# A closing quantisation of y in two engine passes a block instead of four, with other places for the input rows

## What is computed

```python
QMAX, EPS = 7, 1e-8
def fp4_activation(x):
    scale = jnp.max(jnp.abs(x)) / QMAX + EPS
    q = jnp.clip(jnp.round(x / scale), -QMAX, QMAX) * scale
    return x + stop_gradient(q - x)

c = einsum('bct,bcd->bdt', x, w[conditions])      # 128 batches
h = gelu(ternary_linear(c, W1, b1))               # 512 -> 2048
y = ternary_linear(h, W2, b2)                     # 2048 -> 512
out = x + fp4_activation(y)
```

## Time and profile before

| | us |
|---|---|
| median of 3 runs | 1052.09 |
| lowest and highest run | 1050.0, 1052.19 |
| span of the profiled execution | 1048.1 |
| busy in it: PE, DVE, ACT, POOL | 938.5, 668.6, 574.4, 157.7 |
| DMA over the span | 77.89 MB, 74 GB/s on average |
| start of the closing part (first roundings) | 982.2 |

### The profile page before, as it was taken

How to read it: one execution, slowest core, us unless ns; L and a number is a source line. 1 busy time by engine, 2 the same in 40 slices (tenths; PEclk the granted TensorE clock), 3 DMA queues, 4 the chain that set the end, 5 groups by cost and what they waited for, 6 DMA issues and landing times.

```text
span 1048.1 us, 15055 instructions
## 1 busy us (share of the span) xinstructions
PE 938.5 (90%) x5265; PEld 449.2 (43%) x5265; DVE 668.6 (64%) x1029; ACT 574.4 (55%) x721; POOL 157.7 (15%) x213
## 2 busy tenths in 40 slices
PE   0599999999999999999999999999999999999300
PEld 0355444444444444444444444444444444444100
DVE  3599766666566756576666666665666656532698
ACT  3489382827455463728273645647382827354495
POOL 4032303030211203030303011020303030000000
PEclk9899999999999999999999999999999999999755
DMA  6510120301111112102020111121210301115898
GB/s 218 200 44 4 36 56 11 81 10 40 46 44 42 48 40 50 40 25 65 10 66 23 41 45 45 40 50 40 48 42 10 80 10 40 40 40 188 297 384 333
DMA packets 40480, 77.89 MB, mean 74 GB/s; under 512 B 3840, under 2 KB 4240, under 8 KB 39952
## 3 DMA queue, kind: packets, MB, share of 16 engines
q1 hardware_dynamic: 36192, 73.47, 23.9%
q0 software_dynamic: 4096, 3.94, 1.3%
q10 hardware_dynamic: 176, 0.27, 0.1%
HBM read 60.89 MB, written 16.78 MB: 74 GB/s over the span
## 4 chain that ended last, share of the span: by engine, by line
PE 76%; issue 11%; DVE 7%; ACT 2%; POOL 2%; DMA 1%; SPq 0%; POOLq 0%; DVEq 0%; ACTq 0%
PE ps L427 38%; PE ps L439 35%; PE ps L415 2%; DVE wts L947 1%; DVE y L941 1%; PE ps L457 1%; ACT y L636 1%; POOL ws L339 1%; DVE st L697 1%; DMA yx<-in_x 1%; DVE y L937 1%; DVE y L811 0%; DVE wts L808 0%; DMA condb<-in_itok_B 0%; DVE yc L947 0%
## 5 line engine op out<-in xcount | busy, mean ns | idle before, releaser
L427 PE MATMUL ps<-yc,wts 128*128 128x512 f16 x2048 | 447.3, 379 | 0.3 <-ACT g L568 0.3
L439 PE MATMUL ps<-wts 128*128 128x512 f16 x1920 | 419.3, 379 | 0.7 <-ACT wts L592 0.7
L427 PEld LDWEIGHTS ps<-yc,wts 128*128 128x128 f16 x2048 | 199.6, 98 | 238.5 <-ACT g L568 0.8
L439 PEld LDWEIGHTS ps<-wts 128*128 128x128 f16 x1920 | 185.8, 98 | 220.4 <-ACT wts L592 0.9
L730 DVE SCALAR_TENSOR_TENSOR wts<-g,st,wts 128x512 f16<-128x512 f32 x256 | 186.4, 749 | 143.5 <-ACT wts L573 141.8
L568 ACT ACTIVATE g<-ps,b1t,st 128x512 f32<-128x512 f32 x256 | 197.9, 773 | 116.7 <-PE ps L427 106.4
L573 ACT ACTIVATE wts<-g,st 128x512 f16<-128x512 f32 x256 | 181.0, 713 | 0.0
L555 ACT ACTIVATE xs<-yx,st 128x2048 f16<-128x2048 f32 x28 | 56.1, 2002 | 144.2 <-DVE st L765 144.2
L361 POOL PARTITION_ALL_REDUCE st<-st x46 | 21.5, 468 | 669.5 <-DVE st L699 414.3
L339 POOL DMA_INDIRECT wg<-in_L_cond_weights,ids x112 | 106.6, 952 | 41.3 <-issue 28.3
L735 DVE SCALAR_TENSOR_TENSOR y<-ps,st,b2b 128x512 f32 (+1 forms) x56 | 41.9, 748 | 77.8 <-PE ps L439 77.8
(11 more groups left out here) (127 smaller groups left out, 431.9 us busy)
## 6 DMA issues: line engine op xcount, KB each, us to landing
yx<-in_x SPq DMA_DIRECT2D x56, 512.0 KB, 6.0
wts<-in_x SPq DMA_DIRECT2D x9, 1024.0 KB, 8.1
out<-wts SPq DMA_DIRECT2D x6, 1024.0 KB, 6.3
y<-in_L_ffn_W SPq DMA_DIRECT2D x8, 512.0 KB, 8.8
y<-in_L_ffn_W SPq DMA_DIRECT2D x4, 1024.0 KB, 8.0
out<-wts SPq DMA_DIRECT2D x8, 512.0 KB, 5.1
xs<-in_x SPq DMA_DIRECT2D x2, 1024.0 KB, 5.9
yc<-in_x SPq DMA_DIRECT2D x2, 1024.0 KB, 7.8
```

Source lines behind the costliest of these rows:

```text
L427: last = nc.tensor.matmul(psH[:, j % HB, :], T1T[:, k, j * P:(j + 1) * P], csp[:, a, k, :], start=(k == 0 and a == 0), stop=(k == KT - 1 a ...
L439: last = nc.tensor.matmul(psY[:, r % 2, :], hsp[:, a, j, r * P:(r + 1) * P], T2T[:, j, :], start=(j == 0 and a == 0), stop=(j == HT - 1 an ...
```

## The change

The rounded number y*qi + MAGIC, seen as bits, has the whole number q in two's complement in its low 16 bits, as MAGIC's own bits there are zero. The changed kernel reads those 16 bits directly in the final sum, as an int16 at every second place of `y`, so that `whole` and `clipped` go. The clip to 7 goes too: y/scale can't be over 7, since scale is max|y|/7 + EPS. What remains are `rounded` and `added`, with int16 in place of fp16 as `added`'s first operand, at a step of two.

Around it:

- Pieces: block 0 in four quarters (one tile of 512 each), block 1 in two halves, blocks 2 to 15 whole; 20 pieces. VectorE rounds the pieces 0, 1 and 3, ScalarE all others.
- Places: blocks 6 to 11 get the parts of `wts` in another order. Block 6's is free after one quarter of the last product and its load is issued then; 7 and 8 after two, 9 after three, 10 and 11 after all, as before. `APART` is (6, 8, 9, 11).
- Blocks 12 to 15 get places of their own, the y of blocks 0 to 3. SP issues the load of block b + 12 right behind the last store of block b; the wait for a landing is gone.
- One counter `o_stored` for all stores, waited for at the end.
- The memset of `magn` at the kernel's start is gone.

```diff
-        HALVED = (0, 1, 2)
-        PIECES = [(b, slice(m, m + 1)) for b in HALVED for m in (0, 1)] + [(b, slice(0, 2)) for b in range(len(HALVED), NB)]
-        BY_VECTOR = [1, 3, 5, 6] + list(range(8, len(PIECES), 3))
+        ALL = slice(0, 2)
+        CUT = {0: [(slice(m, m + 1), slice(n, n + 1)) for m in (0, 1) for n in (0, 1)],
+               1: [(slice(m, m + 1), ALL) for m in (0, 1)]}
+        PIECES = [(b, m, n) for b in range(NB) for m, n in CUT.get(b, [(ALL, ALL)])]
+        LAST_OF = {b: i for i, (b, _, _) in enumerate(PIECES)}
+        BY_VECTOR = (0, 1, 3)
...
+        def q_piece(b, m, n):
+            return y_piece(b, m, n).bitcast(I16).rearrange("p m n (t w) -> p m n t w", w=2)[:, :, :, :, 0]
+
+        def x_piece(b, m, n):
+            return xtail[b][:, m, n, :]
...
-        xtail += [parts[:, w, 0:2, :, :] for w in range(3)]
-        xtail += [parts[:, 0:2, 2, :, :], parts[:, 0:2, 3, :, :], parts[:, 2, 2:4, :, :]]
+        xtail += [parts[:, 0:2, 0, :, :], parts[:, 2, 0:2, :, :], parts[:, 0:2, 1, :, :]]
+        xtail += [parts[:, 0:2, 2, :, :], parts[:, 2, 2:4, :, :], parts[:, 0:2, 3, :, :]]
+        APART = (6, 8, 9, 11)
         XS = len(xtail)
-        APART = (9, 10)
+        xtail += [place(y[:, b, :, :].rearrange("p r t -> p (r t)")) for b in range(NB - XS)]
...
+            sp.wait_ge(quarters_used, 1)
+            load_tail(6)
             sp.wait_ge(quarters_used, 2)
-            for b in range(6, 9):
-                load_tail(b)
+            load_tail(7)
+            load_tail(8)
...
-            for n, (b, m) in enumerate(PIECES):
-                sp.wait_ge(o_made, n + 1)
-                stored = place_stored[b] if b + XS < NB else o_stored
-                for rows, source in transfers(b, m):
-                    sp.dma_start(out_v[:, rows, :].rearrange("p (m n) t -> p m n t", n=2), source).then_inc(stored, 16)
-                if b >= 1 and m.stop == 2 and b - 1 + XS < NB:
-                    sp.wait_ge(place_stored[b - 1], 32 if b - 1 in HALVED else 16)
-                    load_tail(b - 1 + XS)
+            stores = 0
+            for i, (b, m, n) in enumerate(PIECES):
+                sp.wait_ge(o_made, i + 1)
+                for rows, source, cols in transfers(b, m, n):
+                    sp.dma_start(rows_of(out_v, rows, cols), source).then_inc(o_stored, 16)
+                    stores += 1
+                if i == LAST_OF[b] and b < NB - XS:
+                    load_tail(b + XS)
+            sp.wait_ge(o_stored, 16 * stores)
...
-            rounded(0)
-            for n in range(1, len(PIECES)):
-                if n not in BY_VECTOR:
-                    rounded(n)
-                whole(n - 1)
-            whole(len(PIECES) - 1)
+            for i, piece in enumerate(PIECES):
+                if i not in BY_VECTOR:
+                    nc.scalar.activation(y_piece(*piece), y_piece(*piece), ACT.Identity, scale=qi, bias=magp).then_inc(q_rounded, 1)
...
+            def added(i):
+                b = PIECES[i][0]
+                if i in BY_VECTOR:
+                    dve.wait_ge(q_rounded_vector, BY_VECTOR.index(i) + 1)
+                else:
+                    dve.wait_ge(q_rounded, i + 1 - sum(v < i for v in BY_VECTOR))
+                dve.wait_ge(xt_loaded[b], 32 if b in APART else 16)
+                nc.vector.scalar_tensor_tensor(out=x_piece(*PIECES[i]), in0=q_piece(*PIECES[i]), scalar=qs, in1=x_piece(*PIECES[i]),
+                                               op0=ALU.mult, op1=ALU.add).then_inc(o_made, 1)
 
             dve.wait_ge(q_ready, 1)
-            for n in range(len(PIECES)):
-                if n + 1 in BY_VECTOR:
-                    rounded(n + 1)
-                clipped(n)
-                added(n)
+            for i in range(len(PIECES)):
+                if i == 0:
+                    rounded(0)
+                if i + 1 in BY_VECTOR:
+                    rounded(i + 1)
+                added(i)
```

More of the change, by code:

```diff
@@ L8 @@
 I32 = mybir.dt.int32
+I16 = mybir.dt.int16
 ACT = mybir.ActivationFunctionType
@@ L99, in build, with y_piece @@
         ymax = sb("ymax", [P, NB * RT], FP32)
-        HALVED = (0, 1, 2)
-        PIECES = [(b, slice(m, m + 1)) for b in HALVED for m in (0, 1)] + [(b, slice(0, 2)) for b in range(len(HALVED), NB)]
-        BY_VECTOR = [1, 3, 5, 6] + list(range(8, len(PIECES), 3))
+        ALL = slice(0, 2)
[4 more added lines that the diff above has]
+        BY_VECTOR = (0, 1, 3)
         def y_of(b):
             return y[:, b, :, :] if b < NY else (yx[:, :, :], psEnd[1])[b - NY]
[L111 to L123, removed]
+        def y_piece(b, m, n):
+            return (y_of(b) if b < NY else psEnd[b - NY]).rearrange("p (m n) t -> p m n t", m=2)[:, m, n, :]
+        def q_piece(b, m, n):
+            return y_piece(b, m, n).bitcast(I16).rearrange("p m n (t w) -> p m n t w", w=2)[:, :, :, :, 0]
+        def x_piece(b, m, n):
+            return xtail[b][:, m, n, :]
         xd = yx[:, :, :]
@@ L189, in build @@
         ym, ymr, qs, qi = stat(), stat(), stat(), stat()
-        magp, magn, zero, first_gelu = stat(), stat(), stat(), stat()
+        magp, zero, first_gelu = stat(), stat(), stat()
         ps = pb("ps", [P, HB + 4, T], FP32)
@@ L235, in build @@
         ymax_part, ymax_all, q_ready = sem("ymax_part"), sem("ymax_all"), sem("q_ready")
[L236 to L239, removed]
+        xt_loaded = [sem(f"xt_loaded{b}") for b in range(NB)]
+        q_rounded_vector, q_rounded, o_made = sem("q_rounded_vector"), sem("q_rounded"), sem("o_made")
         o_stored = sem("o_stored")
@@ L269, in _, with transfers, rows_of @@
                 load_half(n, n * HALF + DIRECT * BB)
-            def transfers(b, m):
-                cut = [slice(i, i + 1) for i in range(m.start, m.stop)] if b % XS in APART else [m]
-                return [(slice(b * RT + 2 * c.start, b * RT + 2 * c.stop), x_piece(b, c)) for c in cut]
+            def transfers(b, m, n):
+                cut = [slice(i, i + 1) for i in range(m.start, m.stop)] if b in APART else [m]
+                return [(slice(b * RT + 2 * c.start + n.start, b * RT + 2 * (c.stop - 1) + n.stop), x_piece(b, c, n), n) for c in cut]
+            def rows_of(view, rows, n):
+                return view[:, rows, :].rearrange("p (m n) t -> p m n t", n=n.stop - n.start)
             def load_tail(b):
-                for rows, to in transfers(b, slice(0, 2)):
-                    sp.dma_start(to, x_v[:, rows, :].rearrange("p (m n) t -> p m n t", n=2)).then_inc(xt_loaded[b % XS], 16)
+                for rows, to, n in transfers(b, ALL, ALL):
+                    sp.dma_start(to, rows_of(x_v, rows, n)).then_inc(xt_loaded[b], 16)
             sp.wait_ge(c_made, 2 * NB)
@@ L297, in _ @@
             sp.wait_ge(y_summed, NB * RT)
[L298 to L310 removed]
+            load_tail(10)
+            load_tail(11)
+            stores = 0
[7 more added lines that the diff above has]
+            sp.wait_ge(o_stored, 16 * stores)
         @block.gpsimd
@@ L788, in _ @@
             nc.vector.memset(zero, 0.0).then_inc(zero_made, 1)
-            nc.vector.memset(magn, -MAGIC)
             for c in range(LOADS):
@@ L933, in _, with rounded @@
             nc.vector.reciprocal(qi, qs).then_inc(q_ready, 1)
[L935 to L947, removed]
+            def rounded(i):
+                nc.vector.tensor_scalar(y_piece(*PIECES[i]), y_piece(*PIECES[i]), qi, MAGIC, ALU.mult, ALU.add)\
+                    .then_inc(q_rounded_vector, 1)
+            def added(i):
[6 more added lines that the diff above has]
+                nc.vector.scalar_tensor_tensor(out=x_piece(*PIECES[i]), in0=q_piece(*PIECES[i]), scalar=qs, in1=x_piece(*PIECES[i]),
                                                op0=ALU.mult, op1=ALU.add).then_inc(o_made, 1)
             dve.wait_ge(q_ready, 1)
-            for n in range(len(PIECES)):
-                if n + 1 in BY_VECTOR:
-                    rounded(n + 1)
-                clipped(n)
-                added(n)
+            for i in range(len(PIECES)):
[4 more added lines that the diff above has]
+                added(i)
 _INS = ['x', 'itok_B_1_198', 'L0_cond_weights', 'L0_ffn_W1', 'L0_ffn_b1', 'L0_ffn_W2', 'L0_ffn_b2']
```

## The result

The changed kernel takes 1044.27 us (median of 4 runs, 1043.16 to 1047.25), the kernel before 1051.55 beside it (4 runs, 1050.0 to 1052.19). The ratio is 0.994 with a 95% interval of 0.9928 to 0.9953: 6.3 us less, between 4.9 and 7.6. The forecast was 1045.4, with 1042.3 to 1050.0 around it. The profiled execution of the changed kernel took 1043.87 us, and its span is 1042.1, so 1.8 us lie around a span, not the 4.0 that the forecast took from the median.

What follows compares the result with a forecast made beforehand. VectorE bounded the closing part, then the DMA queues: 984 + 54.0 us for 22.0 MB = 1038.0, plus 2.35 collisions and 1.1 end = 1041.4 span, plus 4.0 around it = 1045.4 us; range 1042.3 to 1050.0.

Steps and rivals of the forecast that it cites:

- The bound before, and the bound after: Closing part: VectorE bounds it before the change, the DMA queues after; VectorE would end at 1022.7 instead of 1043.3.
- VectorE's sum: VectorE's closing work after the change, three roundings and 20 sums at 2.35 us per whole block: 40.5 us in total.
- the gap of 0.03 us: Allowance between successive VectorE operations in the closing part, counted 20 times.
- The 1016 and 1023: Times when VectorE would need the loads of blocks 12 and 15; load 15 landing by about 1007, eight us of cover.
- Rival (d): VectorE's strided int16 sum costs two steps an element, 4.5 us a whole block; time 1065.9 us; chance 0.03.
- The bytes and their rate: DMA queues from 984 on: 22.0 MB at 407 GB/s take 54.0 us, last data packet at 1038.0.
- Rival (b): Queues set the closing part's end, but at a lasting 358 GB/s; time 1050.6 us; chance 0.08.
- Collisions: Closing part's loads and stores meeting: 2.35 us kept as lost, from two stretches before 998.
- Rival (c): Loads and stores meeting early in the closing part: 9.4 MB at 247 GB/s, 38.1 us; time 1058.2 us; chance 0.05.
- SP's line: SP's closing issues cost 0.37 to some 0.5 us each; four more stores, about 2 us, add nothing to the total.
- Around the span: Time outside the profiled span: 4.0 us, from span 1048.1 against median 1052.09, added to the new span.
- Load 6's earlier issue and the memset: Load issued one quarter of the last product earlier, and one memset less at the kernel's start; both costed at nothing.

Runs made afterwards that it cites:

- second run: Kernel before with the sum reading the low 16 bits, no second ScalarE pass, no clip, and VectorE rounding piece 1 alone; 1045.62 us, ratio 0.9953.
- first: Kernel before with the sum reading the low 16 bits, no second ScalarE pass and no clip; pieces, places, waits kept; 1045.53 us, ratio 0.9954.
- last run: Changed kernel with 1.3 MB of x loaded early, block 12's last quarter and blocks 13 to 15 loaded together behind block 3's store; 1042.22 us, ratio 0.9921.
- the one with one reduction: Changed kernel with one extra VectorE reduction of 512 columns ahead of each of the 14 whole sums; 1051.57 us on another chip, ratio 0.9941.

## Why the prediction was right, point by point

**The bound before, and the bound after.** Right. VectorE set the closing part, and the queues took it over: fewer bytes help (9.6 us for 4.2 MB), moving the roundings off VectorE doesn't (second run against first), 8.4 us more work for it doesn't hurt and 24.9 do, as a slack of 16 would have it. VectorE ends 22.0 us earlier in span time (1043.3 to 1021.29), the kernel 6.0: the other 16 us are now SP's blocked issues and its last wait of 10.1 us.

**VectorE's sum.** 40.5 us forecast, 38.0 measured. The operations were sized right (2347 for 2351, 746 for 760, 483 for 480 ns). Wrong was the gap of 0.03 us: sums that wait for nothing overlap, 2.26 us from one to the next. The trace of before could have told: its sum of 2.35 us at 1029.73 is followed at 1032.00 by a rounding that waits for nothing. It cost nothing, being on a slack path. The 1016 and 1023 at which VectorE was said to need blocks 12 and 15 are the ends of these sums by the forecast's own working; their starts would be 1013.2 and 1020.3. Rival (d), two steps an element, is off: 2347 ns. The Trainium skill, "SBUF — State Buffer", section "Door 1: The DMA port swizzle", says how far one can stride in SBUF for free, eight places for bf16. The trace agrees for an int16 at a step of two, 2347 ns; larger steps were not run.

**The bytes and their rate.** 22.0 MB from 984 on at 407 GB/s were forecast; it was 388 x 58.1 = 22.5 MB at 408. The half megabyte more, 1.2 us, is from the start: the closing part began 1.1 us later in this execution (983.3 for 982.2), and loads 10 and 11 0.7 later (980.68 for 980.00). The second run, with the old places and a start at 983.03, has 22.3 MB from 984 on, so that term is hardly an effect of the change. Rival (b), a lasting 358 GB/s, is off in this kernel, 408 for 40 us; with it the rule of 358 for transfers with HBM in the Trainium skill, "SBUF — State Buffer", section "Summary: rules for kernel authors", which the trace does not bear out here either.

**Collisions.** 2.35 us forecast, measured 4 x (1 - 362/408) + 4 x (1 - 379/408) + 4 x (1 - 349/408) = 1.3 us. The mechanism is there, half the size. The forecast took the whole shortfall of two stretches of before for slow packets, though their shares of 0.84 and 0.98, against 1.05 where the queues are full, say that they were partly idle. An estimate that leaves the idle part out, 4 x (0.84/1.05 - 292/407) + 4 x (0.98/1.05 - 283/407), gives 1.3 us. Rival (c), down to 247 GB/s for 38 us, didn't come. It did come for short times: 236 GB/s for 4 us in the last run. The two misses, 1.2 us more and 1.05 less, nearly cancel, which is luck. The span was 1042.1 for 1041.4; of these 0.7 us 0.2 lie in the two, and the rest at the end, where the rate falls to 391 GB/s from 1036 on and to 248 from 1040 to 1041.

**SP's line.** This step was wrong. I reckoned with some 5 MB of stock and a last issue near 1023. In fact SP's issues block: 2.2 us and more for each 1 MB instead of 0.37 once about four whole blocks are on their way. The last issue ended at 1031.56. Load 15 was issued at 997.37, not 994.4, and the sum that needs it starts at about 1019. It costs nothing here: the queues run at 408 or 409 GB/s all through the blocked issues from 996 to 1032.

**Around the span.** 4.0 us were added for it, 1.8 is right. The 4.0 compared the span of one execution with the median of others: in 52 executions of the kernel before, beside the experiments, 1.8 to 2.1 us lie around the span, so the profiled one is the 1050.0, 1.9 above its span and the shortest of them. In the changed kernel the median stands only 0.4 us over the profiled execution. With 1.9 in place of 4.0 the forecast would have been 1043.3, 1.0 us under the measured 1044.27; as it stands, 1045.4, it is 1.1 over. Like with like, the span fell by 6.0 us where 6.7 were forecast.

**What the parts brought.** The likeliest reading: passes 4.8 to 5.3 us, or the clip alone 5.1; places and loads without a wait about 1 (0.9954 to 0.994 and 0.9943), which the intervals do not separate from none but the dry stretch of the second run supports; fine pieces nothing. Load 6's earlier issue and the memset, put at nothing, were not tried by themselves.

## What to carry to other kernels

When an engine bounds a stage, read the DMA rate of that stage before pricing its work: here 22 us less for VectorE were worth 6, because 22 MB at 408 GB/s stood right behind it, and one pass of 0.69 us a block less was already enough. After that, what still helped was to move bytes out of the stage: look for pauses of the queues ahead of it and small tiles that have become free. A wait for a landing on the issuing stream showed as a dry stretch while the queues were nearly empty (27 GB/s for 1 us) and no longer once they were full.

## What the runs showed of the hardware

- SP's DMA issue of 0.37 us grows to 2.2 us and more for 1 MB when the queues are full. In the changed kernel's two profiles, in the two-pass kernel and in the one with one reduction the last landing came 9.9 to 10.1 us after SP's last issue, at 408 GB/s about 4.1 MB; without the late loads 10.5 us, at some 375 GB/s about 3.9; so some four blocks seem to be the most that is on its way. That number is worked out, not read.
- Stores run at 408 GB/s in the changed kernel and at 372 to 392 without the late loads (996 to 1032), with shares of 1.01 to 1.05 in both. Why is open. VectorE's work isn't the cause, as the rate stays 408 or 409 beside it from 996 to 1012 in the changed kernel. That SP's issues are not blocked without the late loads isn't it either: in the kernel before SP waits for VectorE for 15.6 of the 20 us from 1012 to 1032, and the queues move 403 to 410 GB/s there from 1016 on; and with the roundings moved they still move 410 and 409 from 1032 to 1040, when SP has nothing left to issue after 1032.87.
- Stretches with loads beside stores lost 1.3 us (the changed kernel) to 2.8 us (the first run with more loaded early: 392, 312, 288 and 356 GB/s in the four stretches from 984 to 1000), in another place from run to run; part of the larger loss is idle time, with shares of 0.95 and 0.99. Grouping the loads did not change it. The cause wasn't found.
- VectorE instructions that wait for nothing start some 0.09 us before the one ahead of them ends in the records (2.26 from start to start, 2.35 each; reductions of 0.69 take 0.60).
